# Preparing the next batch on GpSimd, and an earlier PSUM copy on VectorE, in the attention of a Trainium2 kernel

## Chip, cores and metric

One NeuronCore of one Trainium2 chip. The metric is the device time of one execution in microseconds. Engine names in the profile: PE is TensorE's matmuls, PEld its weight loads, DVE VectorE, ACT ScalarE, POOL GpSimd, SP SyncE (here only an issuer of DMAs).

## What is computed

Four blocks on x of shape (8, 256, 256): a cross attention, a mixture of experts, a second cross attention and a second mixture of experts. The change touches only the first attention:

```
latn = layernorm(layernorm(x)) * ln2_w + ln2_b        # plain layernorm first, then one with weights
xn   = layernorm(ctx) * ln1_w + ln1_b                 # ctx: (8, 256, 256)
q    = latn @ Wq                                      # 16 heads of 64
k, v = split(concat([xn, latn]) @ Wkv)                # 512 keys per batch
out  = softmax(q k^T / 8) @ v @ Wo
x    = x + out
```

EPS is 1e-5. A layernorm without weights applied twice can be written as one: if v is the variance of a row, the second pass divides by sqrt(v/(v+EPS) + EPS), so both together divide the centred row by sqrt(v*(1+EPS) + EPS*EPS).

## The kernel before

attend_latents handles 8 batches one after the other. Each batch has 8 steps, one for each pair of heads. The engines run their own programs, ordered by hand, and meet through semaphores; each engine executes strictly in the order of its program. All matrix products of fp32 data are made from a high and a low part in fp32r: ScalarE writes the high part, VectorE or GpSimd subtracts it from the full value for the low part.

TensorE's program for step r of batch b is, in order: score(r, 0), turn(previous pair, 2), project_k(next pair), score(r, 1), turn(previous, 3), project_q(next), score(r, 2), turn(r, 0), project_v (of this batch's next group of columns, in steps 6 and 7 of the next batch), score(r, 3), attend(previous), turn(r, 1). A score (lines 297 and 298) makes 128 queries by 512 keys; a turn (line 307) transposes the probabilities by four 128 by 128 blocks into PSUM; attend (lines 321 and 325) needs all four turned copies of its pair. At the end of step 2 project_out multiplies the batch before by Wo. At the end of steps 4 and 5 turn_inputs transposes the normalised inputs of the next batch (xn, line 333) by halves of the model width; it waits for the semaphore normed. In the last batch the parts for a next batch are left out.

ScalarE makes the exponentials (line 435), copies two of the four turned blocks (set_even, line 453), the high parts (set_k, line 418; set_q, line 412; high_kv, line 403; high_o, line 460), and v. VectorE makes the row maxima (maximum, line 603), copies the other two turned blocks (set_odd, line 618), the low parts low_k (line 597) and low_q (line 590), divides the outputs (set_out, lines 625 and 627), and applies the weights of the layernorm to the transposed inputs (fill, line 582). GpSimd splits the weights at the start (lines 220 and 222), and then has only low_o (line 207, one 128 by 256 subtraction a step) and low_kv (line 202, two of 128 by 512 a batch).

The layernorm of the next batch is spread over VectorE's program in 19 parts of two to seven instructions. Part n stands in step n // 4, behind maximum n % 4 of that step, so it fills steps 0 to 4:

```
def between(r, j):
    if last < 2 and 4 * r + j < PARTS:
        prepare(b + 1, 4 * r + j)
```

The parts compute mean and variance (bn_stats, bn_aggr), a reciprocal root by a bit trick and three Newton steps on 4 numbers a partition, the normalised latents and context, then statistics and root again for the latents, and the second normalisation. For batch 0 all parts run at once at the start. Chain is a helper: it lets each instruction wait for the one before on the same engine. The SP queue loads x and ctx for a batch once the batch before is normalised, and at the start the weight pieces.

Of the kernel before, what the change touches and what calls it, by code (L numbers as in the profile page):

```python
# [6 lines left out]
F32 = mybir.dt.float32  # L7
F32R = mybir.dt.float32r
BF16 = mybir.dt.bfloat16
I32 = mybir.dt.int32  # L10
U32 = mybir.dt.uint32
ALU = mybir.AluOpType
# [3 lines left out]
P = 128  # L16
# [25 lines left out]
def wait(eng, sem, value):  # L42

    if not isinstance(value, int) or value > 0:
        eng.wait_ge(sem, value)
# [21 lines left out]
def attend_latents(nc, g, io):  # L67
# [15 lines left out]
    with ExitStack() as ctx:  # L83
        def sb(name, shape, dt=F32):
            return ctx.enter_context(nc.sbuf_tensor(name, shape, dt))
# [5 lines left out]
            return ctx.enter_context(nc.semaphore(name))  # L91


        ctx_in, lat, xn = sb("a_ctx_in", [P, 2, D]), sb("a_lat", [P, 2, D]), sb("a_xn", [P, 4, D])
        stats, mv, rstd = sb("a_stats", [P, 6, 6]), sb("a_mv", [P, 6, 2]), sb("a_rstd", [P, 6])
        var, tmp, guess = sb("a_var", [P, 4]), sb("a_tmp", [P, 4]), sb("a_guess", [P, 4], I32)
        affine, zeros = sb("a_affine", [P, 4, KC]), sb("a_zeros", [P, D])
        full = sb("a_full", [P, KC, N])
# [56 lines left out]
        with nc.Block() as block:  # L155
            @block.sync
            def _(sp):
                def load(b):

                    wait(sp, loaded, 32 * b)  # L160
                    wait(sp, normed, b)
                    sp.dma_start(g.x[:, bass.ds(2 * b, 2), :], x_dram[:, bass.ds(b, 1)]).then_inc(loaded, 16)
                    sp.dma_start(ctx_in[:, :, :], c_dram[:, bass.ds(b, 1)]).then_inc(loaded, 16)

                def load_piece(i):

# [29 lines left out]

            @block.gpsimd
            def _(pool):
                def low_kv(b, bp, kc):

                    pool.wait_ge(kvh_set, KC * b + kc + 1)
                    pool.tensor_tensor(kvT_l[bp][:, kc, :], full[:, kc, :], kvT_h[bp][:, kc, :],  # L202
                                       ALU.subtract).then_inc(kvl_set, 1)

                def low_o(b, r):
                    pool.wait_ge(oh_set, PAIRS * b + r + 1)
                    pool.tensor_tensor(o_l[:, r, :], o_full[r % 4][:, :], o_h[:, r, :], ALU.subtract).then_inc(ol_set, 1)  # L207
# [16 lines left out]
                def step(b, bp, first, last):  # L224
                    for r in range(PAIRS):
                        if r in (5, 6) and last < 2:
                            low_kv(b + 1, 1 - bp, r - 5)
                        if r >= 2:
                            low_o(b, r - 2)
                        elif not first:  # L230
                            low_o(b - 1, PAIRS + r - 2)

                pool.memset(g.ident[:, :], 0.0).then_inc(ident_set, 1)
                pool.wait_ge(ident_set, 1)
# [269 lines left out]

            @block.vector
            def _(dve):
                link = Chain(dve, chain)
                PARTS = 19

                def seed_root(n):  # L510

                    link(dve.tensor_scalar(var[:, 0:n], mv[:, 0:4, 1] if n == 4 else mv[:, 4:6, 1], EPS, None, ALU.add))
                    link(dve.tensor_scalar(guess[:, 0:n], var[:, 0:n].bitcast(I32), 1, None, ALU.logical_shift_right))
                    link(dve.tensor_scalar(guess[:, 0:n], guess[:, 0:n], -1, 0x5f3759df, ALU.mult, ALU.add))

                def newton(n, src, dst, half):


                    if half == 0:
                        link(dve.tensor_tensor(tmp[:, 0:n], src, src, ALU.mult))  # L520
                        link(dve.tensor_tensor(tmp[:, 0:n], tmp[:, 0:n], var[:, 0:n], ALU.mult))
                    else:
                        link(dve.tensor_scalar(tmp[:, 0:n], tmp[:, 0:n], -0.5, 1.5, ALU.mult, ALU.add))
                        link(dve.tensor_tensor(dst, src, tmp[:, 0:n], ALU.mult))

                def prepare(b, part):


                    def rows(t):
                        return g.x[:, bass.ds(2 * b + t, 1), :]  # L530

                    if part == 0:
                        link.restart()
                        dve.wait_ge(loaded, 32 * (b + 1))
                        for t in range(2):
                            dve.bn_stats(stats[:, t, :], rows(t))
                    elif part == 1:
                        for t in range(2, 4):
                            ins = dve.bn_stats(stats[:, t, :], ctx_in[:, t - 2, :])
                        link(ins)  # L540
                    elif part == 2:
                        for t in range(4):
                            ins = dve.bn_aggr(mv[:, t, :], stats[:, t, :])
                        link(ins)
                        seed_root(4)
                    elif part in range(3, 9):
                        newton(4, guess[:, :].bitcast(F32) if part < 5 else rstd[:, 0:4], rstd[:, 0:4], (part - 3) % 2)
                    elif part == 9:
                        for t in range(2):
                            ins = dve.tensor_scalar(lat[:, t, :], rows(t), mv[:, t, 0:1], rstd[:, t:t + 1],  # L550
                                                    ALU.subtract, ALU.mult)
                        link(ins)
                    elif part == 10:

                        wait(dve, inputs_turned, KC * b)
                        for t in range(2):
                            dve.tensor_scalar(xn[:, t, :], ctx_in[:, t, :], mv[:, 2 + t, 0:1],
                                              rstd[:, 2 + t:3 + t], ALU.subtract, ALU.mult)
                    elif part == 11:
                        for t in range(2):  # L560
                            ins = dve.bn_stats(stats[:, 4 + t, :], lat[:, t, :])
                        link(ins)
                        for t in range(2):
                            ins = dve.bn_aggr(mv[:, 4 + t, :], stats[:, 4 + t, :])
                        link(ins)
                        seed_root(2)
                    elif part in range(12, 18):
                        newton(2, guess[:, 0:2].bitcast(F32) if part < 14 else rstd[:, 4:6], rstd[:, 4:6], part % 2)
                    elif part == 18:
                        for t in range(2):  # L570
                            ins = dve.tensor_scalar(xn[:, 2 + t, :], lat[:, t, :], mv[:, 4 + t, 0:1],
                                                    rstd[:, 4 + t:5 + t], ALU.subtract, ALU.mult)
                        ins.then_inc(normed, 1)

                def fill(b, kc):

# [24 lines left out]
                def maximum(b, r, j):  # L601
                    dve.wait_ge(s_done, 4 * (PAIRS * b + r) + j + 1)
                    dve.tensor_reduce(negmax[:, j:j + 1], scores[j % 2][:, :], AX.X, ALU.max,  # L603
                                      negate=True).then_inc(max_set, 1)
# [27 lines left out]
                    dve.tensor_tensor(rows, rows, q_p[:, :].rearrange("p (t d) -> p t d", t=2), ALU.add).then_inc(added, 1)  # L632

                def step(b, bp, first, last):
                    def between(r, j):
                        if last < 2 and 4 * r + j < PARTS:
                            prepare(b + 1, 4 * r + j)

                    for r in range(PAIRS):
                        prev, nxt = before(b, r, first), after(b, r, bp, last)  # L640
                        maximum(b, r, 0)
                        if prev:
                            invert(*prev)
                        between(r, 0)
                        maximum(b, r, 1)
                        if nxt:
                            low_k(*nxt[:2])
                        if prev:
                            set_odd(*prev, 3)
                        between(r, 1)  # L650
                        maximum(b, r, 2)
                        if nxt:
                            low_q(*nxt[:2])
                        between(r, 2)
                        maximum(b, r, 3)
                        if prev:
                            set_out(*prev)
                        set_odd(b, r, 1)
                        between(r, 3)
                        if r == 2 and not first:  # L660
                            add(b - 1)
                        if r in (4, 5) and last < 2:
                            fill(b + 1, r - 4)

                dve.memset(g.eps[:, :], EPS)
                for part in range(PARTS):
                    prepare(0, part)
                dve.wait_ge(const_in, 64)
                for kc in range(KC):
                    fill(0, kc)  # L670
# [1545 lines left out]
```

## Time and profile before

| what | value |
|---|---|
| median of 3 runs | 1681.82 us (1680.61 to 1682.15) |
| the profiled execution, its time | 1679.78 us |
| its span in the trace | 1678.1 us |
| first attention in it | 0 to about 728 us |
| TensorE, VectorE, ScalarE, GpSimd busy | 88%, 61%, 52%, 27% of the span |

Busy shares are averages over four blocks that have different limits. Times inside the trace are microseconds from the start of the span; PEclk is the share of full clock granted to TensorE in a stretch, 1.00 being 2.4 GHz and 0.50 being 1.2 GHz. A step of a batch is marked by the start of its first matmul of line 297.

### The profile page before, as it was taken

Reading aid. Unit: us, or ns where it says so; the run is one execution under the profiler, and the core shown is the slowest. Engines: PE = TensorE matmul, PEld = TensorE weight load, DVE = VectorE, ACT = ScalarE, POOL = GpSimd, SP = SyncE. Lnnn points to the kernel's source line nnn. Section 1 sums busy time; section 2 is a strip of 40 time slices with the busy share of each in tenths; the row PEclk is TensorE's granted clock in tenths of the full one; section 3 lists DMA queues with packets and bytes.
Section 4 is the critical chain, followed back from the end, with each engine's and each line's share of the span. In section 5 each row is a group of like instructions: output and inputs, shape, how many; then the busy total and the mean of one; then the engine's idle time right before and its main releaser. Section 6 shows DMA issues by size and latency. Waiting matters only on the chain. (4 is left out here: it accounts for less than half of the span.)

```text
span 1678.1 us, 28402 instructions
## 1 busy us (share of the span) xinstructions
PE 1479.7 (88%) x9884; PEld 1201.2 (72%) x9884; DVE 1017.5 (61%) x2142; ACT 879.1 (52%) x2200; POOL 458.8 (27%) x395
## 2 busy tenths in 40 slices
PE   4899999999999999958999996699999629999996
PEld 3678777777777778747888885365655518888885
DVE  5877777777777876755311115377777654444452
ACT  2676767676767777835211113366666214445442
POOL 6110101010101010033200006222322015777874
PEclk9999999999999999977999998599999659999998
DMA  3300000000000000012489883000000223445442
GB/s 115 108 14 1 14 1 14 2 14 2 14 2 14 1 1 1 1 38 98 135 296 318 300 287 60 19 14 7 12 3 2 88 81 101 119 121 126 122 116 33
DMA packets 72255, 118.17 MB, mean 70 GB/s; under 512 B 6864, under 2 KB 52944, under 8 KB 72112
## 3 DMA queue, kind: packets, MB, share of 16 engines
q1 hardware_dynamic: 61408, 99.66, 18.4%
q0 software_dynamic: 10704, 16.65, 4.9%
q8 instruction: 83, 1.36, 0.3%
q14 instruction: 60, 0.49, 0.1%
HBM read 97.68 MB, written 18.61 MB: 69 GB/s over the span
## 5 line engine op out<-in xcount | busy, mean ns | idle before, releaser
L435 ACT ACTIVATE a_p<-a_s,a_negmax 128x512 f32<-128x512 f32 x256 | 176.0, 688 | 157.6 <-DVE a_negmax L603 115.9
L603 DVE TENSOR_REDUCE a_negmax<-a_s 128x1 f32<-128x512 f32 x256 | 176.1, 688 | 47.0 <-PE a_s L298 36.8
L207 POOL TENSOR_TENSOR a_o_l<-a_o,a_o_h 128x256 fp32r<-128x256 f32 x64 | 47.0, 735 | 559.8 <-ACT a_o_h L460 559.8
L1495 ACT ACTIVATE h_probs<-h_scores,h_negmax 128x256 f32<-128x256 f32 x256 | 117.8, 473 | 88.6 <-DVE h_negmax L1662 88.6
L307 PEld LDWEIGHTS a_t<-ident,a_p 128*128 128x128 f32 x1024 | 121.1, 140 | 52.9 <-issue 17.9
L307 PE MATMUL a_t<-ident,a_p 128*128 128x128 f32 x1024 | 157.5, 277 | 0.7 <-DVE a_pT L618 0.7
L1907 POOL TENSOR_TENSOR n_w_l<-n_raw,n_w_h 128x768 fp32r<-128x768 f32 x64 | 118.3, 1849 | 74.7 <-ACT n_w_h L1950 74.7
L597 DVE TENSOR_TENSOR a_k_hl<-a_k_p,a_k_hl 64x512 fp32r<-64x512 f32 x128 | 88.1, 688 | 71.6 <-ACT a_k_hl L418 70.5
L325 PE MATMUL a_out_p<-a_pT,a_v 128*64 128x256 f32 x1024 | 124.7, 386 | 0.0
L297 PE MATMUL a_s<-a_k_hl,a_q_hh 128*128 128x512 f32 x256 | 108.5, 424 | 8.9 <-ACT a_p L435 7.2
L1662 DVE TENSOR_REDUCE h_negmax<-h_scores 128x4 f32<-128x1024 f32 x64 | 78.1, 1221 | 55.3 <-PE h_scores L1589 55.3
L2088 DVE TENSOR_TENSOR n_hidden<-n_up,n_silu 128x512 f32<-128x512 f32 x64 | 44.3, 692 | 97.9 <-PE n_up L1992 93.6
L1600 PEld LDWEIGHTS h_turned<-ident,h_probs 128*128 128x128 f32 x512 | 55.8, 143 | 66.1 <-issue 48.0
L298 PE MATMUL a_s<-a_k_hl,a_q_l 128*128 128x512 f32 x256 | 101.3, 396 | 0.0
L412 ACT ACTIVATE a_q_hh<-a_q_p 64x256 fp32r<-64x256 f32 x256 | 95.9, 375 | 2.3
L325 PEld LDWEIGHTS a_out_p<-a_pT,a_v 128*64 128x64 f32 x1024 | 67.8, 136 | 38.4 <-issue 10.7
L2091 DVE TENSOR_TENSOR n_hid_l<-n_hidden,n_hid_h 128x512 fp32r<-128x512 f32 x64 | 63.3, 989 | 44.7 <-ACT n_hid_h L1971 44.7
L618 DVE COPY a_pT<-a_t 128x512 f32<-128x512 f32 x128 | 87.8, 686 | 2.6 <-PE a_t L307 0.7
L1600 PE MATMUL h_turned<-ident,h_probs 128*128 128x128 f32 x512 | 73.6, 286 | 13.5 <-DVE h_probsT L1672 13.4
L1966 ACT ACTIVATE n_silu<-n_gate 128x512 f32<-128x512 f32 x64 | 38.3, 598 | 84.2 <-PE n_gate L1992 84.2
L1334 DVE TENSOR_TENSOR e_hidden<-m_up,e_silu 128x512 f32<-128x512 f32 x31 | 21.4, 692 | 100.3 <-PE m_up L1069 100.3
L255 PE MATMUL a_v_p<-a_w_h,a_kvT_h 128*128 128x256 f32 x256 | 77.8, 304 | 4.8 <-POOL a_kvT_l L202 3.7
(325 smaller groups left out, 4294.3 us busy)
## 6 DMA issues: line engine op xcount, KB each, us to landing
e_w_in<-in_L_ffn_gate_up_proj SPq DMA_DIRECT2D x31, 1024.0 KB, 7.1
n_raw<-in_L_ffn_w SPq DMA_DIRECT2D x64, 384.0 KB, 3.0
e_w_out<-in_L_ffn_down_proj SPq DMA_DIRECT2D x31, 512.0 KB, 5.2
rows_in<-a_zeros SPq DMA_DIRECT2D x1, 3968.0 KB, 14.6
e_rows<-rows_in SPq DMA_DIRECT2D x31, 128.0 KB, 5.0
rows_out<-e_result POOLq DMA_DIRECT2D x31, 128.0 KB, 4.8
x<-in_x SPq DMA_DIRECT2D x8, 256.0 KB, 2.8
a_ctx_in<-in_ctx SPq DMA_DIRECT2D x8, 256.0 KB, 3.1
```

What stands on the lines that cost most here:

```text
L297: pe.matmul(scores[j % 2][:, :], q_hh[r % 2][:, h, rows], k_hl[r % 2][h][:, :], start=True, stop=False)
L298: pe.matmul(scores[j % 2][:, :], q_l[r % 2][:, h, rows], k_hl[r % 2][h][:, :], start=False, stop=True).then_inc(s_done, 1)
L307: ins = pe.transpose(turned_p[j % 2][:, c, :], probs[j][:, c * P:(c + 1) * P], g.ident[:, :])
L325: ins = pe.matmul(out_p[h * DH:(h + 1) * DH, 0, :], v[r // 2 % 2][:, c, at:at + DH], probsT[r % 2][h][:, c, :], start=(c == 0), stop=(c == ...
L412: ins = act.activation(q_hh[r % 2][half, h, :], q_p[halves[h], 0:S], ACT.Copy, scale=QSCALE)
L435: act.activation(probs[j][:, :], scores[j % 2][:, :], ACT.Exp, bias=negmax[:, j:j + 1], accum_out=total[:, r % 2, j % 2, j // 2:j // 2 + 1 ...
L597: ins = dve.tensor_tensor(k_hl[r % 2][h][halves[1 - h], :], k_p[half, :], k_hl[r % 2][h][half, :], ALU.subtract)
L603: dve.tensor_reduce(negmax[:, j:j + 1], scores[j % 2][:, :], AX.X, ALU.max, negate=True).then_inc(max_set, 1)
L618: dve.tensor_copy(probsT[r % 2][j // 2][:, :, P:2 * P], turned_p[1][:, :, :]).then_inc(odd_set, 1)
L1495: ins = act.activation(probs[s % 4][:, j, :], scores[s % 2][:, j // 2, j % 2, :], ACT.Exp, bias=negmax[:, s % 4, j:j + 1], accum_out=total ...
L1600: ins = pe.transpose(turned_p[i][:, j, c, :], probs[s % 4][:, 2 * i + j, c * P:(c + 1) * P], g.ident[:, :])
L1907: pool.tensor_tensor(w_l[c % RAWS][:, :], raw[c % RAWS][:, :], w_h[c % RAWS][:, :], ALU.subtract).then_inc(wl_set, 1)
```

## The change

The normalisation of batches 1 to 7 moves from VectorE to GpSimd: centre(b + 1) is run after low_o in step 2, scale(b + 1) after low_o in step 3. GpSimd sums rows by halving: 128 + 128 columns, then 64, and so on to 1, for four rows a partition at once. The two layernorms of the latents become one. VectorE keeps the normalisation of batch 0 (normalise_first), also in the folded form. The inputs are loaded into one tile `both` (4 x 256 a partition), and x once more into its own place, so there are three DMAs a batch where there were two. In VectorE's step, set_odd(previous pair, 3) now stands ahead of low_k.

```diff
-                    sp.dma_start(g.x[...], x_dram[...]).then_inc(loaded, 16)
-                    sp.dma_start(ctx_in[:, :, :], c_dram[...]).then_inc(loaded, 16)
+                    sp.dma_start(both[:, 0:2, :], c_dram[...]).then_inc(loaded, 16)
+                    sp.dma_start(both[:, 2:4, :], x_dram[...]).then_inc(loaded, 16)
+                    sp.dma_start(g.x[...], x_dram[...]).then_inc(loaded, 16)
...
+                def root(n, dst, var, tmp, guess):
+                    link(pool.tensor_scalar(guess, var.bitcast(I32), -0.5, float(0x5f3759df), ALU.mult, ALU.add))
+                    src = guess.bitcast(F32)
+                    for i in range(3):
+                        link(pool.tensor_tensor(tmp, src, src, ALU.mult))
+                        link(pool.tensor_tensor(tmp, tmp, var, ALU.mult))
+                        link(pool.tensor_scalar(tmp, tmp, -0.5, 1.5, ALU.mult, ALU.add))
+                        link(pool.tensor_tensor(dst, src, tmp, ALU.mult))
+                        src = dst
+
+                def total_of(rows, half):
+                    n = D // 2
+                    link(pool.tensor_tensor(half[:, :, 0:n], rows[:, :, 0:n], rows[:, :, n:D], ALU.add))
+                    while n > 1:
+                        n //= 2
+                        link(pool.tensor_tensor(half[:, :, 0:n], half[:, :, 0:n], half[:, :, n:2 * n], ALU.add))
+                    return half[:, :, 0]
+
+                def centre(b):
+                    link.restart()
+                    pool.wait_ge(loaded, 48 * (b + 1))
+                    link(pool.tensor_scalar(mean[:, :], total_of(both[:, :, :], halved[:, :, :]), 1.0 / D, None, ALU.mult))
+                    wait(pool, inputs_turned, KC * b)
+                    link(pool.tensor_tensor(xn[:, :, :], both[:, :, :], mean[:, :].unsqueeze(2).to_broadcast([P, 4, D]), ALU.subtract))
+                    link(pool.tensor_tensor(both[:, :, :], xn[:, :, :], xn[:, :, :], ALU.mult))
+
+                def scale(b):
+                    sums = total_of(both[:, :, :], halved[:, :, :])
+                    pool.tensor_scalar(var[:, 0:2], sums[:, 0:2], 1.0 / D, EPS, ALU.mult, ALU.add)
+                    link(pool.tensor_scalar(var[:, 2:4], sums[:, 2:4], (1.0 + EPS) / D, EPS * EPS, ALU.mult, ALU.add))
+                    root(4, rstd[:, :], var[:, :], tmp[:, :], guess[:, :])
+                    pool.tensor_tensor(xn[:, :, :], xn[:, :, :], rstd[...].to_broadcast([P, 4, D]), ALU.mult).then_inc(normed, 1)
...
+                        if last < 2:
+                            if r == 2:
+                                centre(b + 1)
+                            if r == 3:
+                                scale(b + 1)
...
-                def prepare(b, part):
...
+                def normalise_first():
+                    dve.wait_ge(loaded, 48)
+                    for t in range(4):
+                        ins = dve.bn_stats(stats[:, t, :], both[:, t, :])
...
+                    for t in range(4):
+                        ins = dve.tensor_scalar(xn[:, t, :], both[:, t, :], mv[:, t, 0:1], rstd[:, t:t + 1], ALU.subtract, ALU.mult)
+                    ins.then_inc(normed, 1)
...
                         maximum(b, r, 0)
                         if prev:
                             invert(*prev)
-                        between(r, 0)
                         maximum(b, r, 1)
+                        if prev:
+                            set_odd(*prev, 3)
                         if nxt:
                             low_k(*nxt[:2])
-                        if prev:
-                            set_odd(*prev, 3)
-                        between(r, 1)
                         maximum(b, r, 2)
```

## Rows read from the trace of the kernel before

**Rows 1.** The page: busy time of each engine and its share of the span.
```profile
PE 1479.7 (88%) x9884; PEld 1201.2 (72%) x9884; DVE 1017.5 (61%) x2142; ACT 879.1 (52%) x2200; POOL 458.8 (27%) x395
```

**Rows 2.** Windows (stretch, length, busy PE, PEld, DVE, ACT, POOL, PEclk, DMA): batches.
```profile
33.38:116.47 83.09, 76.44 (x512) 60.40 (x511) 68.74 (x150) 60.66 (x150) 19.72 (x14) 0.98 0.22 71
116.47:637.11 520.64, 500.00 (x3507) 402.12 (x3506) 404.48 (x943) 373.93 (x925) 50.55 (x60) 1.00 0.02 6
...
33.38:40.53 7.15, 6.41 (x42) 5.53 (x41) 5.87 (x13) 5.55 (x14) 7.07 (x4) 1.00 0.31 99
```

**Rows 3.** Windows over steps of batch 7, batch 1 and batch 3.
```profile
637.11:670.96 33.85, 33.85 (x249) 28.49 (x248) 22.23 (x42) 23.38 (x58) 2.20 (x3) 1.00 0.00 1
670.96:689.63 18.67, 18.67 (x134) 15.11 (x133) 13.57 (x25) 14.96 (x38) 1.46 (x2) 1.00 0.01 1
152.05:171.25 19.20, 19.20 (x138) 15.47 (x137) 15.48 (x38) 14.15 (x35) 1.47 (x2) 1.00 0.01 1
...
171.25:182.02 10.77, 10.12 (x73) 7.94 (x72) 8.51 (x18) 8.77 (x22) 2.00 (x2) 1.00 0.16 50
182.02:201.47 19.45, 19.04 (x135) 15.19 (x134) 14.54 (x28) 16.03 (x42) 2.76 (x3) 1.00 0.01 1
366.36:377.57 11.21, 9.65 (x69) 7.61 (x67) 8.18 (x16) 8.60 (x23) 1.46 (x2) 1.00 0.01 3
```

**Rows 4.** Waits of TensorE, 0 to 722 us: total us, times, longest.
```profile
PE a_out_p L321 <- DVE a_pT L618: 13.3, 20, 0.8
```

**Rows 5.** Timeline of VectorE in step 5 of batch 1 (start, us).
```profile
176.74 1.39 DVE L597 TENSOR_TENSOR a_k_hl<-a_k_p,a_k_hl 64x512 fp32r<-64x512 f32 x2 [1.75 <-ACT a_k_hl L418]
```

**Rows 6.** Timeline of the start and of batch 0.
```profile
4.26 0.75 DVE L536 BATCH_NORM_STATS2 a_stats<-x 128x6 f32<-128x256 f32 x2 [3.32 <-DMA a_ctx_in<-in_ctx]
...
9.11 0.73 DVE L550 TENSOR_SCALAR a_lat<-x,a_mv,a_rstd 128x256 f32<-128x256 f32 x2
9.88 1.88 DVE L557 TENSOR_SCALAR a_xn<-a_ctx_in,a_mv,a_rstd 128x256 f32<-128x256 f32 x2
10.04 1.58 POOL L220 CAST a_w_h<-a_raw 128x1536 fp32r<-128x1536 f32 x1 [7.31 <-DMA a_raw<-in_L_xattn_Wkv]
...
18.85 1.09 PE L333 MATMUL a_q_p<-ident,a_xn 128*128 128x128 f32 x4 [18.85 <-DVE a_xn L571]
...
21.79 1.26 POOL L202 TENSOR_TENSOR a_kvT_l<-a_full,a_kvT_h 128x512 fp32r<-128x512 f32 x1 [6.67 <-ACT a_kvT_h L403]
...
25.35 0.76 PE L255 MATMUL a_k_p<-a_kvT_h,a_w_h 128*128 128x512 f32 x1 [3.14 <-issue]
...
41.43 2.23 DVE L514 TENSOR_SCALAR a_guess<-a_guess 128x4 int32<-128x4 int32 x1
...
45.25 0.50 PE L297 MATMUL a_s<-a_k_hl,a_q_hh 128*128 128x512 f32 x1 [2.18 <-ACT a_p L435]
```

**Rows 7.** Windows: TensorE's clock after two idle times.
```profile
46.24:49.65 3.41, 3.41 (x15) 2.96 (x14) 3.31 (x6) 2.76 (x6) 2.00 (x1) 0.50 1.08 386
...
720.12:725.85 5.73, 3.41 (x29) 3.44 (x30) 0.85 (x2) 0.42 (x1) 0.72 (x1) 1.00 0.00 0
```

**Rows 8.** Groups of GpSimd by line and shape: count, busy us, mean ns.
```profile
L207 POOL TENSOR_TENSOR a_o_l<-a_o,a_o_h 128x256 fp32r<-128x256 f32 x64 | 47.0, 735 | 559.8 <-ACT a_o_h L460 559.8
L1413 POOL TENSOR_SCALAR h_kz<-h_k,h_mask 128x256 f32<-128x256 f32 x32 | 29.0, 922 | 26.1 <-ACT h_k L1483 26.1
...
L222 POOL TENSOR_TENSOR a_w_l<-a_raw,a_w_h 128x1536 fp32r<-128x1536 f32 x4 | 13.9, 3470 | 0.3
```

**Rows 9.** Timeline of GpSimd: batch 7, and a chain of small instructions.
```profile
671.73 0.73 POOL L207 TENSOR_TENSOR a_o_l<-a_o,a_o_h 128x256 fp32r<-128x256 f32 x1 [14.30 <-ACT a_o_h L460]
...
1061.41 0.11 POOL L1440 MEMSET h_bands<- 128x8 f32 x1 [15.17 <-POOLq L2109]
1061.59 0.19 POOL L1441 TENSOR_SCALAR_AFFINE_SELECT h_bands<-h_bands 128x8 f32<-128x8 f32 x1
1061.85 0.19 POOL L1443 TENSOR_SCALAR_AFFINE_SELECT h_bands<-h_bands 128x8 f32<-128x8 f32 x1
```

**Rows 10.** The tile of VectorE's copy, line 618: ns min/median/max, first and last start.
```profile
L618 DVE COPY a_pT<-a_t x128: 678/683/694, 44.3 to 717.0; 128x512 f32<-128x512 f32 x128
```

More of the change, by code:

```diff
@@ L91, in sem @@
             return ctx.enter_context(nc.semaphore(name))
-        ctx_in, lat, xn = sb("a_ctx_in", [P, 2, D]), sb("a_lat", [P, 2, D]), sb("a_xn", [P, 4, D])
-        stats, mv, rstd = sb("a_stats", [P, 6, 6]), sb("a_mv", [P, 6, 2]), sb("a_rstd", [P, 6])
+        both, xn = sb("a_both", [P, 4, D]), sb("a_xn", [P, 4, D])
+        halved = sb("a_halved", [P, 4, D // 2])
+        stats, mv, first_chain = sb("a_stats", [P, 4, 6]), sb("a_mv", [P, 4, 2]), sem("a_first_chain")
+        mean, rstd = sb("a_mean", [P, 4]), sb("a_rstd", [P, 4])
         var, tmp, guess = sb("a_var", [P, 4]), sb("a_tmp", [P, 4]), sb("a_guess", [P, 4], I32)
@@ L158, in load @@
                 def load(b):
-                    wait(sp, loaded, 32 * b)
+                    wait(sp, loaded, 48 * b)
                     wait(sp, normed, b)
+                    sp.dma_start(both[:, 0:2, :], c_dram[:, bass.ds(b, 1)]).then_inc(loaded, 16)
+                    sp.dma_start(both[:, 2:4, :], x_dram[:, bass.ds(b, 1)]).then_inc(loaded, 16)
                     sp.dma_start(g.x[:, bass.ds(2 * b, 2), :], x_dram[:, bass.ds(b, 1)]).then_inc(loaded, 16)
-                    sp.dma_start(ctx_in[:, :, :], c_dram[:, bass.ds(b, 1)]).then_inc(loaded, 16)
                 def load_piece(i):
@@ L198, in _ @@
             def _(pool):
+                link = Chain(pool, chain)
+                def root(n, dst, var, tmp, guess):
[26 more added lines that the diff above has]
+                    root(4, rstd[:, :], var[:, :], tmp[:, :], guess[:, :])
+                    pool.tensor_tensor(xn[:, :, :], xn[:, :, :], rstd[:, :].unsqueeze(2).to_broadcast([P, 4, D]), ALU.mult).then_inc(normed, 1)
                 def low_kv(b, bp, kc):
@@ L506, in _ @@
             def _(dve):
[L507 to L524, printed above, removed]
@@ L526, in prepare @@
-                def prepare(b, part):
[L529 to L573, printed above, removed]
@@ new lines, in normalise_first @@
+                def normalise_first():
+                    link = Chain(dve, first_chain)
+                    dve.wait_ge(loaded, 48)
+                    for t in range(4):
+                        ins = dve.bn_stats(stats[:, t, :], both[:, t, :])
+                    link(ins)
+                    for t in range(4):
+                        ins = dve.bn_aggr(mv[:, t, :], stats[:, t, :])
+                    link(ins)
+                    dve.tensor_scalar(var[:, 0:2], mv[:, 0:2, 1], EPS, None, ALU.add)
+                    link(dve.tensor_scalar(var[:, 2:4], mv[:, 2:4, 1], 1.0 + EPS, EPS * EPS, ALU.mult, ALU.add))
+                    link(dve.tensor_scalar(guess[:, :], var[:, :].bitcast(I32), 1, None, ALU.logical_shift_right))
+                    link(dve.tensor_scalar(guess[:, :], guess[:, :], -1, 0x5f3759df, ALU.mult, ALU.add))
+                    src = guess[:, :].bitcast(F32)
+                    for i in range(3):
+                        link(dve.tensor_tensor(tmp[:, :], src, src, ALU.mult))
+                        link(dve.tensor_tensor(tmp[:, :], tmp[:, :], var[:, :], ALU.mult))
+                        link(dve.tensor_scalar(tmp[:, :], tmp[:, :], -0.5, 1.5, ALU.mult, ALU.add))
+                        link(dve.tensor_tensor(rstd[:, :], src, tmp[:, :], ALU.mult))
+                        src = rstd[:, :]
+                    for t in range(4):
+                        ins = dve.tensor_scalar(xn[:, t, :], both[:, t, :], mv[:, t, 0:1], rstd[:, t:t + 1], ALU.subtract, ALU.mult)
+                    ins.then_inc(normed, 1)
@@ L634, in step @@
                 def step(b, bp, first, last):
-                    def between(r, j):
-                        if last < 2 and 4 * r + j < PARTS:
-                            prepare(b + 1, 4 * r + j)
                     for r in range(PAIRS):
@@ L653, in step @@
                             low_q(*nxt[:2])
-                        between(r, 2)
                         maximum(b, r, 3)
@@ L658, in step @@
                         set_odd(b, r, 1)
-                        between(r, 3)
                         if r == 2 and not first:
@@ L665, in _ @@
                 dve.memset(g.eps[:, :], EPS)
-                for part in range(PARTS):
-                    prepare(0, part)
+                normalise_first()
                 dve.wait_ge(const_in, 64)
```

## Prediction

> **What bounds the kernel now.** I read the page first: TensorE is busy 88% of the span, GpSimd 27% [rows 1]. That is an average over stages, so I cut the first attention (0 to about 728 us of the 1678.1) into its eight batches and a batch into its eight steps of one head pair, marking each step by the first score matmul of line 297. Batch 0 takes 83.09 us, batches 1 to 6 together 520.64, 86.8 each [rows 2]. In batch 7, which has no next batch to prepare, TensorE is busy for every microsecond of its first five steps, 33.85 us for steps 0 to 2 and 18.67 for steps 3 and 4 [rows 3]: there a step runs at TensorE's own pace (9.3 to 9.4, and 15.1 with the output projection in step 2) and VectorE has slack. Batch 1 shows what transposing and projecting the next batch adds: 19.20 for steps 3 and 4, 10.77 for step 5, 19.45 for steps 6 and 7 [rows 3]. What batches 1 to 6 take above these is TensorE waiting, mostly in line 321 for VectorE's copy of the turned probabilities, 20 times, 13.3 us [rows 4]. So TensorE bounds the stage, with short waits for VectorE, and GpSimd is nearly idle between its calls of line 207.
>
> **Part 1, work taken off VectorE.** 48 small instructions a batch go. What this is worth is read from steps that lack them or do not wait for them: 33.85 + 19.20 + 10.77 + 19.45 = 83.27 a batch.
>
> **Part 2, the copy moved ahead of low_k.** In step 5 of batch 1 VectorE waits 1.75 us for ScalarE's half of k, subtracts for 1.39 [rows 5], and only then, at 178.1, makes the copy; TensorE waits up to 0.8 for such a copy [rows 4]. Its input was turned long before, so it will lie inside the wait. Step 5 has this in every batch, with no part of the normalisation in it, so it gives 0.8 more: 82.46 a batch. What is queued behind the copy, low_k, needs ScalarE's half anyway; k is used a step later. Step 7 of batch 3 is 11.21, not 9.4, at the place where the hardware loop turns [rows 3]; I keep these 1.8. Batches 1 to 6: 6 x 82.46 + 1.8 = 496.6, against 520.64, a gain of 24.0.
>
> **Part 3, batch 0.** Here GpSimd still splits weights, and one 4-element instruction of VectorE took 2.23 us while GpSimd worked; ScalarE and then TensorE waited behind it, 2.18 us [rows 6], and the clock halved [rows 7]. All this goes. Batch 0 becomes its short step 0 (7.15 [rows 2]), then about 9.5 + 9.4 + 9.3 (there is no output projection in step 2) and 9.9 + 9.96 + 19.45: 74.7, a gain of 8.4.
>
> **Part 4, the start.** Before, VectorE starts at 4.26, has the first four reciprocal roots at 9.11, then normalises the latents a second time with a chain of its own, and TensorE gets the inputs at 18.85 and projects at 25.35 [rows 6]. The second normalisation is now folded into one formula. A third load of the size of the two must land first; I take 0.65 for it, a fifth of the 3.32 that VectorE waited for two [rows 6], since they overlap. Then 4.85 as before and one instruction more: statistics ready at 9.9, then four instructions a third of a microsecond apart (0.73 for two in line 550). GpSimd's cast, then at about 10.7, will hold the last of them, as one was held (1.88 for two) [rows 6]: ready at 12.5. Transposes, fill, high part: 1.1 + 1.2 + 0.7 gives 15.5; GpSimd is free of piece 0 at 15.8, then two low parts of 1.26, the second after the second transposition: TensorE projects at about 19.2, 6.1 earlier. If two rows are held through the long subtraction as well, it is ready at 16 and the gain is 2.5. The SP queue issues load 1 and piece 2 earlier for it; it holds nothing back.
>
> **Part 5, GpSimd's chain, the cost.** Line 207 takes 735 ns for 256 elements, line 222 takes 3470 for 1536 [rows 8]: 188 ns + 2.14 ns an element. A dependent small instruction starts 0.07 after the end of the one before (1061.59 + 0.19 to 1061.85) [rows 9]. centre: 11 instructions on 3068 elements (halvings of 512 to 4, then subtract and square of 1024): 6.55 + 2.07 + 11 x 0.07 = 9.4 us. scale: 24 on about 2100 elements: 4.5 + 4.5 + 22 x 0.07 = 10.55. With the two calls of line 207 that lie before and between, 21.4. They begin 0.8 into step 3 (671.73 [rows 9] against the step's start, 670.96 [rows 3]) and TensorE wants the result at the end of step 4, 18.67 into step 3 [rows 3]. Done at 22.2, plus about 0.2 of register waits and semaphore: **3.7 us late**, in each of the seven batches that prepare a next one. TensorE is in order and stands in turn_inputs; steps 5 to 7 queue behind. Nothing repays it, since the steps are at TensorE's pace. The Trainium skill says to time GpSimd instructions by the start-to-start spacing, not by the reported duration (Perfetto Trace Analysis, GPSIMD Engine Instruction). This trace agrees: spacing 0.26, duration 0.19 [rows 9]. By durations alone the 33 links would vanish and it would be 1.4 late.
>
> The clock: an idle of 2.18 us was followed by 3.41 us at half of 2.4 GHz; after one of 2.32 (5.73 less 3.41 busy) it stayed full [rows 7]. An idle of 3.7 will nearly always bring the fall. At half clock 3.41 us do the work of 1.7; part of the stretch lies in the idle itself. Between 0 and 1.7 I take 1.4. So 5.1 a batch, 35.7 in all.
>
> VectorE's remaining work beside these 20 us: line 618 reads PSUM and never took more than 694 ns of its median 683, in steps with GpSimd busy and without [rows 10]; held was only what reads and writes SBUF [rows 6]. I cost this at nothing. The Trainium skill says the same: a VectorE instruction with at most one SBUF input and outside the two-port modes does not contend with GpSimd (SBUF — State Buffer, Who interferes with whom).
>
> **Sum.** -6.1 - 8.4 - 24.0 + 35.7 = -2.8 us. The profiled execution took 1679.78 (span 1678.1), so 1677; on the median of 1681.82 it is **1679**. Measurement cannot tell less than 0.2%, 3.4 us, from no change.
>
> **Rivals.**
> 1. Late, but the clock hardly falls: -38.5 + 7 x 3.7 = -12.6, 1669. For it: the idle of 2.32 that cost nothing. Chance 0.22.
> 2. The products and two-operation instructions are dearer than sums. Line 1413, a product, takes 922 ns for 256 elements, 2.87 an element by the same intercept [rows 8]. Two products of 1024 add 1.5 a batch: +10.5, 1689.5, slower. It decides from 0.4 us more a batch on, where the sum passes zero. No row has a product of two tensors. Chance 0.22.
> 3. GpSimd is in time: it would take 17.7 instead of 21.4. Then all 38.5 are gained: 1643. The small instructions would have to cost half of 188 ns; a fill of 8 elements does take 0.11, one that reads and writes 0.19. Chance 0.06.
> 4. VectorE's copies are held by GpSimd after all, as line 514 was: two on TensorE's path in each of two steps, each by 1.2 (half of a 2.4 us instruction): up to +33, 1712. Against it stand [rows 10]. Chance 0.05.
> 5. Moving the copy does nothing, low_k being late in its place: +5.6, 1685. Chance 0.05.
>
> **Numbers.** The sum itself has 0.40; its own range is 1673 to 1686 (start 2.5 or 6.1, lateness within 0.7), of which 0.16 is over 0.2% faster, 0.16 the same, 0.08 slower. Faster: 0.16 + 0.22 + 0.06 = 0.44. Same: 0.16 and 0.03 of rival 5, 0.19. Slower: the rest, 0.37. Range 1664 to 1696: it takes in rivals 1, 2 and 5 and leaves out 3, 4 and the tails.
>
> **What would show it.** VectorE's busy time falls from 67.4 us a batch (404.48 by 6 [rows 2]); its copy no longer follows low_k; batch 7's first five steps stay at 52.5. Steps 1 and 2 lose their waits (9.4 and 15.1), step 5 is 9.9 to 10. GpSimd has about 20 us of new work in steps 3 and 4, linked instructions 0.26 to 0.28 apart. TensorE's transposes of line 333 follow an idle of 3.7 us released by GpSimd, with a half-clock stretch after it. The prediction is wrong if step 4 is not about 13.6 us, if GpSimd's large instructions leave 2.1 ns an element, or if the first projection is not near 19 us.

## The result and the profile after

The changed kernel takes 1668.72 us, the median of 6 runs (1665.18 to 1674.47), against 1681.99 of the kernel before, also 6 runs. The ratio is 0.992, 95% interval 0.9895 to 0.9946: 13 us or 0.8% faster. The forecast of 1679 was too high by 10 us, inside its range of 1664 to 1696; faster had the largest chance, 0.44. The profiled execution took 1667.16 us, its span is 1665.4.

Where the 12.7 us between the two spans lie, first the batches. These are windows of the changed kernel, columns as in [rows 2] and [rows 3]; now line 345 is the first score matmul and marks the steps.

```profile
30.80:108.56 77.76, 75.03 (x512) 60.78 (x511) 55.59 (x102) 61.27 (x150) 35.85 (x49) 0.98 0.23 80
108.56:624.95 516.39, 497.03 (x3507) 407.58 (x3506) 352.70 (x655) 375.03 (x925) 147.19 (x270) 0.99 0.03 9
624.95:658.83 33.88, 33.88 (x250) 28.51 (x249) 22.23 (x42) 23.39 (x58) 2.20 (x3) 1.00 0.01 1
658.83:677.50 18.67, 18.67 (x135) 15.11 (x133) 13.59 (x25) 15.17 (x38) 1.47 (x2) 1.00 0.00 1
```

Batch 0 begins at 30.80 instead of 33.38: 2.6 gained. It takes 77.76 instead of 83.09: 5.3. Batches 1 to 6 take 516.39 instead of 520.64 [rows 2]: 4.3. Batch 7's first five steps are 52.55, as before [rows 3]. All that follows gives the remaining half microsecond. VectorE's load fell from 404.48 to 352.70 us in the six batches, 8.6 a batch, and GpSimd's rose from 50.55 to 147.19, 16.1 a batch: the work was moved at nearly twice its price. TensorE hardly won from it, and the next windows show why. The first is steps 3 and 4 of batch 2, the second its step 5, the third step 5 of batch 1.

```profile
228.69:250.43 21.74, 19.33 (x138) 15.53 (x137) 14.74 (x27) 15.72 (x39) 18.10 (x38) 1.00 0.01 1
250.43:260.25 9.82, 9.82 (x74) 8.04 (x72) 7.20 (x14) 7.22 (x18) 1.50 (x2) 1.00 0.27 83
164.40:175.36 10.96, 10.96 (x73) 8.97 (x71) 7.28 (x14) 8.05 (x20) 1.29 (x1) 0.89 0.25 73
```

Steps 3 and 4 take 21.74 where 19.20 was possible [rows 3]; TensorE is idle for 2.41 of them. Step 5 is 9.82 where the clock stays full. In batch 1 it is 10.96, TensorE busy throughout, with a mean granted clock of 0.89: part of it ran at 1.2 GHz instead of 2.4. TensorE's waits between 60 and 722 us (engine, line, released by; total, times, longest):

```profile
PE a_q_p L381 <- POOL a_xn L240: 16.5, 7, 2.4
PE a_v_p L303 <- POOL a_kvT_l L245: 3.8, 7, 0.6
...
PE a_out_p L369 <- DVE a_pT L622: 0.8, 1, 0.8
```

The 20 waits for VectorE's copy, 13.3 us [rows 4], have shrunk to one. In their place stand seven for GpSimd's last instruction, 16.5 us, 2.36 each. The chain that is late, in batch 1, as GpSimd's timeline (start, us):

```profile
143.19 0.74 POOL L250 TENSOR_TENSOR a_o_l<-a_o,a_o_h 128x256 fp32r<-128x256 f32 x1 [14.51 <-ACT a_o_h L508]
143.89 1.29 POOL L218 TENSOR_TENSOR a_halved<-a_both 128x512 f32<-128x512 f32 x1
145.25 2.86 POOL L221 TENSOR_TENSOR a_halved<-a_halved 128x256 f32<-128x256 f32 x7
148.20 0.23 POOL L229 TENSOR_SCALAR a_mean<-a_halved 128x4 f32<-128x4 f32 x1
148.51 1.89 POOL L232 TENSOR_TENSOR a_xn<-a_both,a_mean 128x1024 f32<-128x1024 f32 x1
150.48 1.90 POOL L233 TENSOR_TENSOR a_both<-a_xn 128x1024 f32<-128x1024 f32 x1
152.45 0.73 POOL L250 TENSOR_TENSOR a_o_l<-a_o,a_o_h 128x256 fp32r<-128x256 f32 x1
...
158.26 0.20 POOL L209 TENSOR_TENSOR a_tmp<-a_guess 128x4 f32<-128x4 f32 x1
158.54 0.20 POOL L210 TENSOR_TENSOR a_tmp<-a_tmp,a_var 128x4 f32<-128x4 f32 x1
...
161.62 1.89 POOL L240 TENSOR_TENSOR a_xn<-a_xn,a_rstd 128x1024 f32<-128x1024 f32 x1
```

TensorE's transposes start at 163.66, after an idle of 2.31. A small instruction is 0.20 long and 0.28 after the one before, as costed; the three of 1024 elements take 1.89, not 2.38. The start, by the same view:

```profile
5.48 1.40 DVE L559 BATCH_NORM_STATS2 a_stats<-a_both 128x6 f32<-128x256 f32 x4 [4.55 <-DMA x<-in_x]
...
10.39 5.71 DVE L576 TENSOR_SCALAR a_xn<-a_both,a_mv,a_rstd 128x256 f32<-128x256 f32 x4
10.51 1.62 POOL L263 CAST a_w_h<-a_raw 128x1536 fp32r<-128x1536 f32 x1 [7.80 <-DMA a_raw<-in_L_xattn_Wkv]
12.22 3.42 POOL L265 TENSOR_TENSOR a_w_l<-a_raw,a_w_h 128x1536 fp32r<-128x1536 f32 x1
...
22.76 0.77 PE L303 MATMUL a_k_p<-a_kvT_h,a_w_h 128*128 128x512 f32 x1 [3.14 <-issue]
```

VectorE's four last instructions take 5.71 us with GpSimd's two lying over them, and TensorE projects at 22.76, only 2.6 earlier than before [rows 6]. That GpSimd is the cause is tested below.

### The profile page after: what moved, and what is told of

Its sections match the earlier page's. It is cut to its first block and busy times, and to the rows that moved or that the text cites. A ratio compares the mean times of both kernels' runs of the same rounds, so it can differ in the third digit from the quotient of the medians.

```text
span 1665.4 us, 28264 instructions
## 1 busy us (share of the span) xinstructions
PE 1474.3 (89%) x9884; PEld 1207.8 (73%) x9884; DVE 949.4 (57%) x1786; ACT 881.1 (53%) x2200; POOL 571.1 (34%) x640
## 5 line engine op out<-in xcount | busy, mean ns | idle before, releaser
L601 DVE TENSOR_TENSOR a_k_hl<-a_k_p,a_k_hl 64x512 fp32r<-64x512 f32 x128 | 88.2, 689 | 16.4 <-ACT a_k_hl L466 13.3
L1667 DVE COPY h_probsT<-h_turned 128x512 f32<-128x512 f32 x128 | 81.3, 676 | 0.9 <-PE h_turned L1595 0.7
```

The source lines that it names most:

```text
L601: ins = dve.tensor_tensor(k_hl[r % 2][h][halves[1 - h], :], k_p[half, :], k_hl[r % 2][h][half, :], ALU.subtract)
```

## The experiments

All are edits of the changed kernel unless said otherwise. The ratio is always to the kernel before, run on the same chip; its 95% interval stands in brackets. Each time is the median of 5 to 7 executions, but for the one marked as a single one.

**The changed kernel again.** No edit.

> The changed kernel itself beside the others on the same chip: 1665 to 1674, the differences being the number of idles of 2.4 us that are followed by a half-clock stretch (4 of 7 in the profiled execution, each worth about 1.5 us).

1670.42 us, ratio 0.9928 (0.9902 to 0.9954). The idles and clock falls are the same as in the first trace: steps 4 of 12.3 to 12.8, and a longer step 5 in four of seven batches.

**GpSimd one step earlier.**

```diff
-                            if r == 2:
+                            if r == 1:
                                 centre(b + 1)
-                            if r == 3:
+                            if r == 2:
                                 scale(b + 1)
```

> centre and scale one step earlier (steps 1 and 2). Theory A (the lateness of GpSimd's chain is all that is left of the cost): steps 4 go from 12.45 to 9.9 us and the half-clock stretches behind the idle go too, 7 x 2.55 + 4 x 1.6 = 24 us less than the changed kernel, about 1645. Rival B (GpSimd's long instructions slow the others by contention, so the lateness only moves): steps 1 and 2 get longer than 9.4 and 15.1 and the time stays above 1660.

1648.81 us, ratio 0.9808 (0.9782 to 0.9835), 22 us under the changed kernel on the same chip and near the expected 1645. Windows of batch 0, of batches 1 to 6, and of steps 3 and 4 and step 5 of batch 1:

```profile
31.36:105.19 73.83, 73.25 (x512) 59.59 (x511) 55.41 (x102) 61.14 (x150) 35.29 (x49) 1.00 0.25 82
105.19:602.57 497.38, 491.24 (x3507) 403.99 (x3506) 351.72 (x655) 374.67 (x925) 147.07 (x270) 1.00 0.03 9
139.06:158.17 19.11, 19.11 (x139) 15.55 (x137) 13.99 (x26) 15.60 (x39) 9.92 (x26) 1.00 0.14 43
158.17:167.99 9.82, 9.82 (x74) 8.05 (x72) 7.71 (x16) 7.31 (x18) 2.01 (x2) 1.00 0.00 0
```

GpSimd's chain in batch 1, its first and last instruction, and TensorE's transposes:

```profile
125.27 1.29 POOL L218 TENSOR_TENSOR a_halved<-a_both 128x512 f32<-128x512 f32 x1
...
149.06 1.89 POOL L240 TENSOR_TENSOR a_xn<-a_xn,a_rstd 128x1024 f32<-128x1024 f32 x1
...
157.81 0.60 PE L381 MATMUL a_q_p<-ident,a_xn 128*128 128x128 f32 x4
```

GpSimd's work is the same (147.07), the idle is gone and with it every clock fall in these batches: 497.38 against 516.39, and 73.83 against 77.76 in batch 0. One step earlier in the program is 15.2 us in time, because step 2 is the long one: centre begins 20.1 us into batch 1 (125.27) instead of 35.3 (143.89), and the chain ends 6.9 us before TensorE wants it. Contention as the cause (rival B) falls. The calls stand in steps 1 and 2 of GpSimd's program, but low_o holds them back, so that the chain runs while TensorE is in steps 2 and 3 and the start of step 4. By the starts of their matmuls these steps took 15.10, 9.28 and 9.83. Steps 2 and 3 of batch 7, where there is no chain, take 15.10 and 9.28, and step 4 of batch 1 took 9.91 in the kernel before: none is longer with the chain.

**Only the order of copy and low_k, in the kernel before.**

```diff
+                        if prev:
+                            set_odd(*prev, 3)
                         if nxt:
                             low_k(*nxt[:2])
-                        if prev:
-                            set_odd(*prev, 3)
```

> The kernel before with only the copy moved ahead of low_k. Theory A (both parts matter): TensorE's 20 waits for the copy, 13.3 us, go, but the late last part of the normalisation in step 4 stays: 1668 to 1672. Rival C (the copy's wait is only a sign of VectorE being full; the wait moves to k or to the exponentials): within 3 us of the kernel before.

1663.61 us, ratio 0.989 (0.9859 to 0.992), below the expected 1668 to 1672. This one reordering, with all normalisation left on VectorE, has a median 7 us under the whole change on the same chip (1670.42). The intervals overlap, so the size of that lead is uncertain; the traces of the two agree with it, batches 0 to 6 taking 586.5 us here and 594.3 there, after a start that is 2.7 later. Its windows of batch 0 and batches 1 to 6, and TensorE's waits:

```profile
33.54:114.38 80.84, 74.99 (x512) 59.35 (x511) 68.28 (x150) 60.98 (x150) 19.64 (x14) 1.00 0.22 73
114.38:620.00 505.62, 496.28 (x3507) 403.73 (x3506) 405.31 (x943) 373.99 (x925) 50.55 (x60) 1.00 0.02 7
```

```profile
PE a_v_p L255 <- POOL a_kvT_l L202: 8.4, 7, 1.3
PE a_s L297 <- ACT a_p L435: 2.7, 3, 1.5
...
PE a_out_p L321 <- DVE a_pT L618: 0.8, 1, 0.8
```

505.62 against 520.64 with VectorE as loaded as before (405.31). The 13.3 us of waits for the copy are down to 0.8; the wait for GpSimd's low part of the inputs in step 6 grew from 3.7 to 8.4. So the wait did not move to k or to the exponentials (rival C falls). The late normalisation in step 4 that I expected to stay went as well: steps 4 of batches 1 to 6 take 9.81 to 9.99, where they took 9.89 to 10.57 before. That is part of why it came out faster than expected.

**The changed kernel with the old order.**

```diff
                         maximum(b, r, 1)
-                        if prev:
-                            set_odd(*prev, 3)
                         if nxt:
                             low_k(*nxt[:2])
+                        if prev:
+                            set_odd(*prev, 3)
                         maximum(b, r, 2)
```

> The changed kernel with low_k ahead of the copy again. Theory A: VectorE has slack everywhere but in step 5, and there the idle of TensorE in front gives it time to catch up, so at most 0.8 a batch: 0 to 5 us over the changed kernel, 1669 to 1674. Rival D (the order is what brought the gain): back to 1680.

1673.32 us, ratio 0.9937 (0.9914 to 0.9961). Rival D falls. It is 3 us above the changed kernel, well within both intervals. In its trace batches 0 to 6 take 596.5 us against 594.2, of which 1.6 is a fall of the clock where the hardware loop turns; whether the order is worth the less than 1 us that is left is open.

**The old order with GpSimd early**, the edit of the run before and the one step earlier together, beside a second run of the early kernel with the copy first.

> centre and scale in steps 1 and 2, and low_k ahead of the copy again. By the prediction's part 2 TensorE waits 0.8 for the copy in step 5 of seven batches, whoever normalises: 5 to 6 us over the run with the copy first. If the wait came from VectorE's normalisation or from a step that began late, steps 5 stay at 9.8 and the times are equal.

> centre and scale in steps 1 and 2 with the copy first, again, beside the other on the same chip: 1647 to 1651.

1647.75 (ratio 0.9793, 0.9767 to 0.982) with the old order and 1646.55 (0.98, 0.9772 to 0.9829) with the copy first: equal. Batch 0, batches 1 to 6, and step 5 of batch 1 with the old order:

```profile
31.14:104.99 73.85, 73.37 (x512) 59.49 (x511) 55.41 (x102) 60.59 (x150) 35.59 (x49) 1.00 0.25 83
104.99:604.18 499.19, 493.80 (x3507) 404.61 (x3506) 351.70 (x655) 374.26 (x925) 147.20 (x270) 1.00 0.03 9
157.97:167.92 9.95, 9.95 (x74) 7.97 (x72) 7.84 (x16) 7.50 (x19) 2.01 (x2) 1.00 0.01 2
```

Step 5 is 9.95, not 10.77, though the order is that of before. Batches 1 to 6 take 499.19, and 499.29 in the run with the copy first beside it. VectorE's first row maximum in step 5 of batch 1, in the kernel before and here:

```profile
173.65 0.68 DVE L603 TENSOR_REDUCE a_negmax<-a_s 128x1 f32<-128x512 f32 x1
...
159.54 0.68 DVE L607 TENSOR_REDUCE a_negmax<-a_s 128x1 f32<-128x512 f32 x1
```

Before, it came 2.40 us after the start of the step (171.25), here 1.57 after it (157.97). The wait of up to 0.8 in step 5 thus needed both: VectorE 0.8 behind when the step began, and the copy behind low_k. Moving the copy alone takes it away too: step 5 of batch 1 is 9.84 with all normalisation on VectorE.

**One more instruction in GpSimd's chain.**

```diff
                     link(pool.tensor_tensor(both[:, :, :], xn[:, :, :], xn[:, :, :], ALU.mult))
+                    link(pool.tensor_tensor(both[:, :, :], xn[:, :, :], xn[:, :, :], ALU.mult))
```

> The changed kernel with the square in centre made twice, 1.96 us more of GpSimd a batch. If the lateness passes straight into the time, step 4 goes from 12.45 to 14.4 and TensorE's idle from 2.4 to 4.3, after which the clock falls in seven batches instead of three or four: 13.7 + 5 = 18 to 19 us over the changed kernel, about 1688. If there is slack that absorbs it, less than 5.

1694.06 us, ratio 1.0064 (1.0043 to 1.0085): by the ratios 23 to 24 us over the changed kernel, and slower than the kernel before. TensorE's wait, and step 5 of batches 1 and 2:

```profile
PE a_q_p L382 <- POOL a_xn L241: 30.3, 7, 4.4
```

```profile
169.04:180.57 11.53, 11.53 (x72) 9.37 (x71) 7.26 (x14) 8.06 (x20) 1.29 (x1) 0.84 0.27 70
257.61:269.02 11.41, 11.41 (x73) 9.29 (x71) 7.27 (x14) 7.96 (x20) 1.50 (x2) 0.85 0.22 71
```

The waits grew by 13.8, which is 7 x 1.97: the instruction passes into the time whole. The clock now falls after all seven idles, and step 5 is 11.4 to 11.6 in every batch instead of 9.82. In the traces steps 4 and 5 of the seven batches are together 20.2 us longer than in the changed kernel, near the expected 18 to 19, and 1.6 more is a fall of the clock at the turn of the hardware loop. What is left of the 23 to 24 lies behind these batches. From the start of batch 7 on, all kernels do nearly the same work, and it took between 1038.6 and 1051.0 us in their profiled executions. That spread goes with one long stretch at 1.2 GHz that begins 400 to 410 us after the start of batch 7: it is 31 and 34 us long in the two executions of 1040.6 and 1038.6, 41 us in the five of 1040.5 to 1045.2, and 55 us in the four of 1048.8 to 1051.0. The kernel before does not fit this row (58 us, 1041.0). What lengthens the stretch was not pursued.

**The price of a GpSimd instruction.** Seven instructions on scratch data in batch 7, where GpSimd is idle; `both` as sum of itself and xn, then xn times xn, the same two into an fp32r tile, then 512 elements as a product of two tiles, of one with itself, and of one with a broadcast.

```diff
+                            link(pool.tensor_tensor(both[:, :, :], both[:, :, :], xn[:, :, :], ALU.add))
+                            link(pool.tensor_tensor(both[:, :, :], xn[:, :, :], xn[:, :, :], ALU.mult))
...
+                            link(pool.tensor_tensor(both[:, 0:2, :], both[:, 0:2, :], xn[:, 0:2, :], ALU.mult))
+                            link(pool.tensor_tensor(both[:, 0:2, :], xn[:, 0:2, :], xn[:, 0:2, :], ALU.mult))
+                            link(pool.tensor_tensor(both[:, 0:2, :], xn[:, 0:2, :], mean[:, 0:2].unsqueeze(2).to_broadcast([P, 2, D]), ALU.mult))
```

> The changed kernel with seven more GpSimd instructions in batch 7, where GpSimd is idle, on scratch data that no result uses. They measure what sets the 1.89 us of a 1024-element instruction, against 2.36 by the line of the kernel before. If a repeated or a broadcast operand makes it cheap, two different tiles take 2.3 to 2.4 and the others 1.9; if the output's type does, the fp32r outputs take 2.36 and all fp32 outputs 1.9; if neither, all take 1.9.

A single execution, 1674.19 us. GpSimd's timeline:

```profile
668.00 2.39 POOL L282 TENSOR_TENSOR a_both<-a_both,a_xn 128x1024 f32<-128x1024 f32 x1
670.47 1.90 POOL L283 TENSOR_TENSOR a_both<-a_xn 128x1024 f32<-128x1024 f32 x1
...
677.77 2.40 POOL L285 TENSOR_TENSOR a_kvT_l<-a_both,a_xn 128x1024 fp32r<-128x1024 f32 x1
680.25 1.89 POOL L287 TENSOR_TENSOR a_kvT_l<-a_xn 128x1024 fp32r<-128x1024 f32 x1
...
687.02 1.29 POOL L290 TENSOR_TENSOR a_both<-a_both,a_xn 128x512 f32<-128x512 f32 x1
688.40 1.04 POOL L291 TENSOR_TENSOR a_both<-a_xn 128x512 f32<-128x512 f32 x1
689.52 1.04 POOL L292 TENSOR_TENSOR a_both<-a_xn,a_mean 128x512 f32<-128x512 f32 x1
```

Two different operands cost what the line of [rows 8] says, 2.39, whatever the operation and the output's type. The same operand twice, or a value broadcast along the row, costs 1.66 ns an element (1.89 less 1.04 over 512) and a fixed 0.19. What counts is the operand and not the tile: the first halving (line 218 above) adds two halves of one tile and takes 1.29 for 512 elements, the price of two tiles.

**The first weight piece held back.**

```diff
+                pool.wait_ge(normed, 1)
                 split_piece(0)
```

> The changed kernel with GpSimd's first weight piece held back until VectorE has normalised batch 0. If the 5.71 us of VectorE's four last instructions are GpSimd's doing, they take 1.4, TensorE projects at 19.3 instead of 22.76, and the time falls by 3.4 us. If not, the start is later by the held piece, up to 5 us slower.

1662.93 us, ratio 0.9881 (0.9859 to 0.9902). The start:

```profile
10.52 1.38 DVE L577 TENSOR_SCALAR a_xn<-a_both,a_mv,a_rstd 128x256 f32<-128x256 f32 x4
11.96 1.46 POOL L263 CAST a_w_h<-a_raw 128x1536 fp32r<-128x1536 f32 x1 [9.24 <-DVE a_xn L577]
...
19.49 0.77 PE L304 MATMUL a_k_p<-a_kvT_h,a_w_h 128*128 128x512 f32 x1 [4.07 <-POOL a_kvT_l L245]
```

The four instructions take 1.38 when GpSimd is still, and TensorE projects at 19.49, 3.3 earlier. So GpSimd's two instructions were the cause of the 5.71. The median fell by more than that, 6 to 8 us by time and ratio; in the trace the start gives 3.3, batches 0 to 6 give 1.4 (the clock fell after three idles instead of four), and the rest is equal.

**Both edits**, earlier steps and the held piece.

> centre and scale in steps 1 and 2 and the first piece held back: 3.4 us under the run with the earlier steps alone, about 1645.

1645.17 us, ratio 0.9768 (0.9744 to 0.9793): the lowest median of all, 2.3% under the kernel before and about 1.5% under the changed one. Its interval overlaps those of the runs with the earlier steps alone, so the step from them rests on the traces: batch 0 begins at 27.57 instead of 31.36, and batches 0 to 6 take 571.4 against 571.2.

## Why the prediction came out as it did

The picture was right: TensorE sets the pace, the waits for the copy go, and GpSimd's chain ends after TensorE wants it, in each of seven batches, with the clock falling behind some of the idles. The sign of the sum was right and its size, -2.8, was a fifth of the 13 measured. All three signs that it named for being wrong came: step 4 is 12.45, not 13.6; GpSimd's three instructions of 1024 elements take 1.66 ns an element, not 2.1; the first projection comes at 22.76, not near 19. In its own terms, with the run that has GpSimd in time as the measure of what lateness costs: the start gave 2.6 instead of 6.1, batch 0 without lateness 9.3 instead of 8.4, batches 1 to 6 without lateness 23.3 instead of 24.0, and the lateness took back 22.9 instead of 35.7. Part by part:

**Part 5, the lateness, was the mis-sized term.** I costed three instructions of 1024 elements by lines that read two different operands; with a repeated or broadcast operand they take 0.49 less each. That is 1.5, against the 1.3 between 3.7 and the measured 2.36; the other errors nearly cancel. Over seven batches it is 10 us. The run with one instruction more shows that this term goes into the time one for one, so the size of the error is the size of what was missing. Small instructions and their links were right within 0.02. The clock, 1.4 a batch, cost 1.3 to 1.6 (steps 4 and 5 together) where it fell, but it fell after four of seven idles in the profiled execution, not after nearly all: about 0.8 a batch. Together 5.1 a batch became 2.5 for step 4 (12.45 against 9.91) and 0.8, about 13 us less over seven batches. **Rival 1** (late, but the clock hardly falls) gave 1669, the measured number, by luck: it kept the full 3.7 of lateness, which was 2.36, and put the clock at nothing, which cost 0.8 a batch, and it kept the 6.1 of the start.

**Rival 2**, dearer products, is refuted: a product of two tiles takes 1.29 for 512 elements, as a sum does. The 922 ns of line 1413 belong to another form, a tensor with one scalar per partition, and say nothing of these products. **Rival 3**, GpSimd in time, was not met here, but its 1643 for that case was tested by the run with earlier steps: 1648.8 and 1646.6, and its batches 1 to 6 took 497.4 against my 496.6. The pace without trouble was read rightly. Most of the rest is the start. **Rival 4**: VectorE's copies were not held by GpSimd's 16 us more a batch: line 622 has a median of 681 ns and never took more than 692, where line 618 had 683 and 694.

**Part 4, the start**, took its other end: the second of the four instructions was held through the cast and the third, 3.58 us long, through the subtraction; the inputs were ready at 16.1 and 2.6 was gained, where I had chosen 6.1 and kept 2.5 as the bound. The third load took 1.2 us more, not 0.65, and the cast came only 0.5 later. Holding GpSimd back gives 19.49, near my 19.2.

**Part 2 counted its last 0.8 on top of part 1, and part 1 already holds it.** The total 82.46 a batch was right, but I gave 0.8 of it to the order of the copy alone. The run with the old order and GpSimd early has nearly the same batches (82.4 by its batch 1). The two parts do not add: freeing VectorE or moving the copy each removes the same 13 us of waits. Alone, the order takes the kernel before to 1663.6; the relocation takes it to 1648 with either order if GpSimd is in time; relocated too late, it gives part of that back. **Part 3** was right: batch 0 without lateness is 73.8, against 74.7.

Open is whether the order matters in the kernel as changed, why the clock fell after some idles of 2.3 to 2.4 us and not after others, and why the stretch at 1.2 GHz behind the attention has different lengths. Two profiled executions of the same kernel, the one with the earlier steps, differ by 5.1 us behind the start of batch 7.

## What to carry to other kernels

Moving work to an idle engine is worth only what its deadline leaves: lay the moved chain's start and length beside the instruction that needs it, and start it a step earlier if they cross, which cost nothing here and gave 22 us. Two edits that remove the same wait don't add up; before relocating work from a busy engine, try whether the one consumer that waits can be served first from the same engine. Here a lateness in front of TensorE, which had no slack behind it, was paid in full, and part of it again by the clock.

## What the runs showed of the hardware

- A GpSimd tensor_tensor that reads the same operand twice, or has one operand broadcast along the row, is faster than one that reads two different operands: 1.90 against 2.39 us for 1024 elements, 1.04 against 1.29 for 512. Two halves of one tile count as different: 1.29.
- After idles of 2.3 to 2.4 us TensorE's clock sometimes fell to half for 3.41 us and sometimes not, in one and the same execution: the idle of 2.31 before 163.66 was followed by a slow step, the idle of 2.41 before 250.02 was not. After idles of 4.3 to 4.4 us it fell every time, seven of seven. Where the hardware loop turns, behind batch 3, the idle is 1.6 to 1.9 us, and the clock fell after it in five of the twelve traces.
- VectorE's TENSOR_SCALAR from SBUF to SBUF was held by GpSimd as before: four of 256 elements took 5.71 us beside it and 1.38 alone. The copies from PSUM were not: a median of 681 ns and at most 692. The Trainium skill (SBUF — State Buffer, Who interferes with whom) says that `tensor_scalar` can enter two-port modes and then contend with GpSimd, and that a VectorE instruction with at most one SBUF input outside these modes does not contend. The trace agrees with both: the first were held, the second were not.
